# A hybrid attention, Mamba and FP4 feed-forward block on one core: set-up merged with the first front, and two products added on GpSimd in 22 of 64 scan units

## The reference, cut to what matters

```python
x = x + attn_a(_layernorm(x))     # 16 heads, latent width 32, rope, causal softmax
x = x + ffn(_layernorm(x))        # gate, up, down (704 wide), rows and weights in FP4 blocks of 16
x = x + attn_b(_layernorm(x))     # two state-space scans (forward, backward), merge, gate
x = x + ffn(_layernorm(x))
# attn_b, one direction; 512 inner channels, 16 states:
dA = exp(dt[..., None] * A);  dBu = dt[..., None] * B_ssm[:, :, None, :] * xc[..., None]
h = dAt * h + dBut                # scan over the 512 tokens, for each channel and state
y = einsum('bdn,bn->bd', h, ct)   # product with C, summed over the 16 states
```

## Time and profile before

| | us |
|---|---|
| median of the runs | 4221.96 |
| the profiled execution | 4215.24 |
| its span, first to last instruction | 4213.5 |
| TensorE busy | 3521.7 (84%) |
| VectorE busy | 3054.1 (72%) |
| ScalarE busy | 2036.8 (48%) |
| GpSimd busy | 1927.2 (46%) |
| first scan starts at | 427.6 |
| mean granted TensorE clock | 0.948 |

### The profile page before, as it was taken

One profiled execution on the slowest core, in us unless ns is written; L12 is line 12 of the kernel. 1 busy time (PEld: TensorE's weight loads), 2 busy tenths in 40 slices (PEclk: granted clock), 3 DMA queues, 4 the chain that ended last, 5 costly groups with the idle time before them and its releaser, 6 DMA issues.

```text
span 4213.5 us, 41483 instructions
## 1 busy us (share of the span) xinstructions
PE 3521.7 (84%) x13488; PEld 1871.2 (44%) x13488; DVE 3054.1 (72%) x4294; ACT 2036.8 (48%) x3852; POOL 1927.2 (46%) x1154
## 2 busy tenths in 40 slices
PE   5886798789988898879988899888988899879657
PEld 5553354245543454435543455434544355434214
DVE  3243768877687867877788776878678777887993
ACT  0354464635645455534655346544555346463441
POOL 0100744546444454445545464544544454453760
PEclk9997899999999999999999999999999999999998
DMA  3002544744446444364436444464454645364780
GB/s 84 1 1 79 190 148 130 248 166 159 142 139 237 143 142 165 137 231 138 152 133 214 157 162 147 143 233 137 136 167 147 220 143 156 128 219 145 268 275 5
DMA packets 203816, 649.64 MB, mean 154 GB/s; under 512 B 34253, under 2 KB 45520, under 8 KB 197456
## 3 DMA queue, kind: packets, MB, share of 16 engines
q1 hardware_dynamic: 203600, 646.98, 45.8%
HBM read 595.52 MB, written 51.38 MB: 154 GB/s over the span
## 4 chain that ended last, share of the span: by engine, by line
PE 48%; DVE 17%; issue 17%; ACT 11%; POOL 6%; SPq 1%; DMA 1%; POOLq 0%; DVEq 0%; ACTq 0%
PE banks L1268 18%; PE banks L1512 9%; DVE banks L844 7%; PE banks L1449 6%; PE banks L1297 5%; PE banks L1273 5%; ACT banks L1234 4%; DVE sb_arena L851 4%; PE banks L1425 3%; POOL sb_arena L980 3%; DVE sb_arena L772 2%; ACT sb_arena L1017 2%; SPq L427 1%; POOL sb_arena L892 1%; ACT sb_arena L1020 1%
## 5 line engine op out<-in xcount | busy, mean ns | idle before, releaser
L980 POOL TENSOR_TENSOR sb_arena<-sb_arena 128x1024 f32<-128x1024 f32 x512 | 1210.2, 2365 | 807.6 <-PE banks L1512 543.6
L844 DVE TENSOR_TENSOR_SCAN banks<-banks,sb_arena 128x512 f32<-128x512 f32 x1024 | 1197.9, 1215 | 212.3 <-ACT banks L1234 163.2
L1512 PE MATMUL banks<-sb_arena,sb_ident 128*128 128x512 f32 x2048 | 1041.0, 636 | 335.4 <-DVE sb_arena L851 266.0
L1234 ACT ACTIVATE banks<-sb_arena,sb_neg_a 128x512 f32<-128x512 f32 x1024 | 665.3, 682 | 1062.1 <-DVE sb_arena L851 1053.5
L1512 PEld LDWEIGHTS banks<-sb_arena,sb_ident 128*128 128x128 f32 x2048 | 386.6, 201 | 824.4 <-DVE sb_arena L851 434.1
L1017 ACT ACTIVATE sb_arena<-banks 128x512 f32<-128x512 f32 (+4 forms) x752 | 381.1, 519 | 582.8 <-PE banks L1273 389.1
L851 DVE TENSOR_TENSOR sb_arena<-banks,sb_arena 128x512 f32<-128x512 f32 x1024 | 650.5, 676 | 0.0
L1273 PE MATMUL banks<-sb_ident,sb_arena 128*128 128x128 f32 (+1 forms) x2082 | 343.8, 287 | 219.3 <-ACT sb_arena L1017 85.6
L1273 PEld LDWEIGHTS banks<-sb_ident,sb_arena 128*128 128x128 f32 (+1 forms) x2082 | 244.2, 145 | 429.7 <-ACT sb_arena L1017 156.7
L723 DVE TENSOR_REDUCE sb_nmax<-banks 128x1 f32<-128x512 f32 (+3 forms) x352 | 222.9, 636 | 290.9 <-PE banks L1452 289.4
L1449 PE MATMUL banks<-sb_arena 128*128 128x384 f32 (+3 forms) x1024 | 358.7, 461 | 0.7 <-issue 0.7
(11 more groups left out here) (126 smaller groups left out, 4027.3 us busy)
## 6 DMA issues: line engine op xcount, KB each, us to landing
sb_arena<-rows_bc SPq DMA_DIRECT2D x1024, 512.0 KB, 4.5
kept_xc<-sb_arena SPq DMA_DIRECT2D x16, 1024.0 KB, 5.0
kept_z<-sb_arena SPq DMA_DIRECT2D x16, 1024.0 KB, 4.4
sb_arena<-kept_z SPq DMA_DIRECT2D x64, 256.0 KB, 5.0
sb_arena<-kept_xc SPq DMA_DIRECT2D x64, 256.0 KB, 4.9
kept_zs<-sb_arena SPq DMA_DIRECT2D x8, 1024.0 KB, 6.6
sb_arena<-kept_zs SPq DMA_DIRECT2D x8, 1024.0 KB, 9.7
sb_xin<-in_x SPq DMA_DIRECT2D x8, 512.0 KB, 7.6
```

Of the source, the lines that this page charges most:

```text
L844: v.tensor_tensor_scan(factors, factors, products, 0.0, ALU.mult, ALU.add).then_inc(V.sem, V.mark("scan", K, e))
L980: nc.gpsimd.tensor_tensor(dBu[K % SLOTS], u[:, p % 2].unsqueeze(1).to_broadcast([P, 2, T]), rows_b[K % BS], ALU.mult).then_inc(G.sem, G.ma ...
L1234: nc.scalar.activation(psum[:, e], dt[:, (K // NQ) % 2], ACT.Exp, scale=neg_a[:, s, m, 2 * q + e:2 * q + e + 1]).then_inc(A.sem, A.mark("d ...
L1512: mm = pe.matmul(psum[:, YB], ident[:, :], dBu[K % SLOTS][:, e], start=(q == 0 and e == 0), stop=(q == NQ - 1 and e == 1))
```

## The change

**Set-up.** SyncE issues 19 loads for the folding at once, without waiting for the memsets, on a semaphore of their own (`s_fold`), then `xin`, then 18 loads that the front needs (`s_mid`: feed-forward weights, rope tables and others), then the rest (`s_w`). The folding uses all 128 rows: `rep16` repeats the 16-row latent matrices eight times down the partitions, `heads_of` keeps each head's own block, and with these block-diagonal right sides (`bd`, `bdv`) eight matmuls of 512 columns and four of 128 replace the 160 small ones; three that make the repeated matrices come ahead, and the 32 for the biases stay. The front begins behind the folding and `s_mid`. VectorE and GpSimd do one weight tile, then four visits of the front, six times; TensorE and ScalarE transpose and copy the feed-forward weights after the front's attention, bank by bank, and then do the front's feed-forward and preparation.

**Units 21 to 42 of each batch** (`ADDED`). VectorE still makes both products. GpSimd then adds the second to the first (`add_states`, after the unit's first place of visits), and TensorE waits for that sum and does one matmul instead of two. `SHARED` is empty, so the paths under `shared(K)` are never taken.

**The table** `VISITS` has new numbers: merge 10 places, ffn2 14, latents 16, attention 44, ffn1 11, early 14, late 19; 128 places in all, where there were 123. The visits' contents and their order are the same.

```diff
+ADDED, SHARED = range(21, 43), ()
-    "lat": (1, 2, 2, 2, 1, 0, 3, 2, 4, 2, 0, 2, 0, 5, 0),
-    "att": (0, 2, 2, 1, 1, 1, 2, 1, 0, 3, 1, 0, 2, 1, 4, 4, 1, 0, 0, 2, 1, 1,
-            0, 3, 0, 2, 0, 4, 1, 1, 2, 1, 3, 1, 0, 4, 1, 2, 3, 0, 1, 3, 0, 0, 3),
+    "lat": (4, 0, 0, 5, 0, 1, 1, 2, 1, 1, 5, 0, 2, 3, 0, 1),
+    "att": (0, 3, 2, 0, 2, 0, 2, 0, 4, 0, 3, 0, 2, 1, 0, 1, 2, 1, 1, 2, 2, 2,
+            0, 0, 5, 0, 4, 0, 3, 0, 1, 2, 1, 0, 4, 1, 2, 2, 0, 3, 4, 0, 0, 3),
...
         def _(sp):
+            for dst, src in fold_loads:
+                sp.dma_start(dst, src, allow_slow_non_contiguous=True).then_inc(s_fold, 16)
+            sp.dma_start(xin[:, :, :], x_dram[0]).then_inc(s_xin, 16)
             sp.wait_ge(V.sem, V.at("cleared"))
+            for dst, src in mid_loads:
+                sp.dma_start(dst, src, allow_slow_non_contiguous=True).then_inc(s_mid, 16)
             for dst, src in loads:
                 sp.dma_start(dst, src, allow_slow_non_contiguous=True).then_inc(s_w, 16)
...
+            front = beside(None, 0)
+            advance(front, MERGE_N + 1)
+            v.wait_ge(s_mid, MID)
+            v.wait_ge(A.sem, A.at("w_v"))
             for i in range(3 * CK):
...
+                advance(front, 4)
+            advance(front, LAT_N + ATT_N - 1 - 4 * 3 * CK)
+            v.wait_ge(s_w, LOADED)
...
+            def add_states(K):
+                g.wait_ge(V.sem, V.at("hc", K, 1))
+                nc.gpsimd.tensor_tensor(dBu[K % SLOTS][:, 0], dBu[K % SLOTS][:, 0], dBu[K % SLOTS][:, 1], ALU.add
+                                        ).then_inc(G.sem, G.mark("pair", K))
...
                     advance(side, visits[2 * k])
+                    if added(K):
+                        add_states(K)
...
-                for e in range(2):
-                    pe.wait_ge(V.sem, V.at("hc", K, e))
+                if added(K):
+                    pe.wait_ge(G.sem, G.at("pair", K))
+                last = 0 if added(K) else 1
+                for e in range(last + 1):
...
                     mm = pe.matmul(psum[:, YB], ident[:, :], dBu[K % SLOTS][:, e],
-                                   start=(q == 0 and e == 0), stop=(q == NQ - 1 and e == 1))
+                                   start=(q == 0 and e == 0), stop=(q == NQ - 1 and e == last))
...
-                        for h in range(H):
-                            last = q == 7 and h == H - 1
-                            accumulate(psum[:, (1 + q) % 8, h * L:h * L + L],
-                                       [(wat[:, w * H + h, k * P:k * P + P], qk17[0:HD, w, r * L:r * L + L])],
-                                       *(("w_lat",) if last else ()))
+                        accumulate(psum[:, fold_bank(w, h, k)],
+                                   [(wat[:, CK * w + h, k * P:k * P + P], bd[w].rearrange("p h l -> p (h l)"))],
+                                   "w_lat", w, h, k)
...
+            front = beside(None, 0)
+            advance(front, MERGE_N + LAT_N + ATT_N)
             pe.wait_ge(G.sem, G.at("wq", 2 * CK - 1))
```

More of the change, by code:

```diff
@@ L302, in hybrid_block @@
         lob = area(HD, rows=1)
+        rep16, heads_of = area(P, rows=HD), area(HPC)
+        bd, bdv = [area(HPC, 2 * L), area(HPC, 2 * L)], area(HPC, HD)
         a_log = area(2, DT * DS)
@@ L373, in hybrid_block @@
             ]
[L374 removed]
+        FOLD, MID, LOADED = 16 * len(fold_loads), 16 * len(mid_loads), 16 * len(loads)
         def by_block(ap):
@@ L397, in unit, with added, shared @@
             return b, p, q, p // DT, p % DT
+        def added(K):
+            return K % NU in ADDED
+        def shared(K):
+            return K % NU in SHARED
         def tile_at(t):
@@ L843, in _ @@
                         v.wait_ge(A.sem, A.at("dA", K, e))
-                        v.tensor_tensor_scan(factors, factors, products, 0.0, ALU.mult, ALU.add
-                                             ).then_inc(V.sem, V.mark("scan", K, e))
+                        v.tensor_tensor_scan(products if e == 1 and shared(K) else factors, factors, products, 0.0,
+                                             ALU.mult, ALU.add).then_inc(V.sem, V.mark("scan", K, e))
                     advance(side, visits[2 * k])
-                    for e in range(2):
+                    for e in range(1 if shared(K) else 2):
                         if e == 0:
@@ L987, in _ @@
                                         ).then_inc(G.sem, G.mark("wq", i))
-            drain(beside(None, 0))
+                advance(front, 4)
+            drain(front)
             soft_sums(0)
@@ L1175, in beside @@
                     yield from prep(n)
+            a.wait_ge(s_fold, FOLD)
+            nc.scalar.activation(b_qk[:, :], b_qk[:, :], ACT.Copy, scale=SCALE).then_inc(A.sem, A.mark())
+            for w in range(2):
+                for h in range(2):
+                    for k in range(CK):
+                        a.wait_ge(E.sem, E.at("w_lat", w, h, k))
+                        for r in range(2):
+                            at = h * HPC * L
+                            copy(w_lat[w][r][:, k, at:at + HPC * L].rearrange("p (h l) -> p h l", l=L),
+                                 psum[:, fold_bank(w, h, k)].rearrange("p (h r l) -> p r h l", h=HPC, r=2)[:, r],
+                                 "w_lat", w, h, k)
+            for k in range(CK):
+                a.wait_ge(E.sem, E.at("w_v", k))
+                copy(w_v[:, k], psum[:, 3 + k, 0:C])
+            a.wait_ge(E.sem, E.at("b_lat"))
+            copy(b_lat[:, :], psum[:, 5, 0:4 * MT])
+            a.wait_ge(E.sem, E.at("b_v"))
+            copy(b_v, psum[0:1, 6, 0:C], "w_v")
+            front = beside(None, 0)
+            advance(front, MERGE_N + LAT_N + ATT_N)
             a.wait_ge(s_w, LOADED)
@@ L1231, in factors @@
                     a.wait_ge(G.sem, G.at("edge", K // NQ))
-                if K >= 1:
+                if K >= 1 and e == 1 and shared(K - 1):
+                    a.wait_ge(V.sem, V.at("scan", K - 1, e))
+                elif K >= 1:
                     a.wait_ge(V.sem, V.at("hc", K - 1, e))
@@ L1509, in state_sum @@
                     pe.wait_ge(V.sem, V.at("ycat", g - 1))
-                for e in range(2):
-                    pe.wait_ge(V.sem, V.at("hc", K, e))
+                if added(K):
+                    pe.wait_ge(G.sem, G.at("pair", K))
+                last = 0 if added(K) else 1
+                for e in range(last + 1):
+                    if e == 1 and shared(K):
+                        pe.wait_ge(G.sem, G.at("hc", K))
+                    elif not added(K):
+                        pe.wait_ge(V.sem, V.at("hc", K, e))
@@ new lines, in _ @@
+            pe.wait_ge(A.sem, A.at("w_v"))
+            pe.wait_ge(s_mid, MID)
+            front = beside(None, 0)
+            advance(front, MERGE_N + LAT_N + ATT_N)
+            pe.wait_ge(G.sem, G.at("wq", 2 * CK - 1))
+            for k in range(CK):
+                for i in range(2 * F // P):
+                    c = i // 4
+                    if k >= 1 and i % 4 == 0:
+                        pe.wait_ge(A.sem, A.at("w_gu", k - 1, c))
+                    turn(psum[:, c, (i % 4) * P:(i % 4) * P + P], rows_gu[:, i * C + k * P:i * C + k * P + P],
+                         *(("w_gu", k, c) if i % 4 == 3 or i == 2 * F // P - 1 else ()))
@@ L1559, in _ @@
             pe.wait_ge(A.sem, A.at("set_up"))
-            accumulate(psum[0:17, 7, 0:1], [(e16[:, :], ones[0:1, 0:1])], "set_up")
-            drain(beside(None, 0))
+            pe.wait_ge(s_w, LOADED)
+            drain(front)
             for b in range(B):
```

168 lines of the change are left out of this document (94 added, 74 removed).

## The result

The changed kernel takes 3973.69 us, the median of four runs (3971.57 to 3975.25); the kernel before, run beside it, 4220.5 (4218.95 to 4224.25). The ratio is 0.9414, with a 95% interval of 0.9397 to 0.943. So 247 us are gained where 140 were forecast, and the time lies under the low end of the range, 3990.

What follows compares the result with a forecast made beforehand. TensorE was taken to bound attention, VectorE the bare units, and the head to add its time directly. Gains 88 + 4 + 54 - 6 = 140 us took the median from 4222 to 4082, range 3990 to 4145.

Steps and rivals of the forecast that it cites:

- the head: Set-up and front: faster loads and folding bring the first scan from 427.64 to about 340, 88 us earlier (75 to 98).
- the table: Same visits in 128 places instead of 123: merge stays TensorE-bound, feed-forward VectorE-bound; counted nothing, bounds -5 and +5 a batch.
- the addition: Units 21 to 42: GpSimd's addition replaces one matmul; 54 gained in batches 1 to 6, 4 in batch 0, 6 lost last.
- The attention units: Units 21 to 42, batches 1 to 6: 0.88 us matmul saved against 1.4 us delay; net 9 us a batch.
- the whole 0.88 is gained: Attention units with visits in the second place: TensorE comes later, so no wait; 11 x 0.88 us a batch.
- Batch 0: Attention stands in units 13 to 34, so only 14 of the 22 units save TensorE time: 4 us gained.
- The last batch: Bare units 21 to 42: GpSimd needs 34.3 us per group of eight, more than VectorE; 6 us lost.
- B: Rival in attention: the new wait eats what the matmul gives, batches 0 to 6 unchanged; 4140 us, chance 0.20 (clock included).
- B's second form: Attention's clock falls from 0.98 to 0.88, TensorE's work grows by 14 us a batch; 4166 us, within B's 0.20.
- C: Rival: TensorE's whole time comes out in attention and the table gains 2 us a batch; 3993 us, chance 0.12.
- D: Rival: additions stand behind `make_dBu` on GpSimd, TensorE waits 2.9 us net in every added unit; 4580 us, chance 0.03.
- E: Rival in the head: front waits for loads or tiles stretch it, so 88 becomes 50; 4120 us, chance 0.07.

Runs made afterwards that it cites:

- e2: The changed kernel without GpSimd's addition in any unit, so new head and new table only: 3986.57 us.
- e6: The changed kernel without GpSimd's addition or the wait for it, the product of state 0 left out of the sum in units 21 to 42: 3948.11 us.
- e1: The changed kernel with no addition in any unit and the old table of visits, so the new head alone: 4117.33 us.
- e15: New head, old table, no addition (e1), with all attention visits but the last moved one place, half a unit, later: 4153.11 us.
- e16: New head, new table, no addition (e2), with the attention list likewise one place later: 4242.22 us.
- e3: The changed kernel with the old table of visits, so new head and GpSimd's addition in units 21 to 42: 4146.48 us.
- e8: The changed kernel with the addition made by VectorE, right behind the unit's products, instead of by GpSimd: 4123.55 us.

## Why the prediction was wrong

By the medians, the 247 us are 103 for the head, 131 for the table and 13 for the addition. The forecast of 140 was 88 for the head, nothing for the table and 52 for the addition (4 + 54 - 6). The misses are 15, 131 and -39: the table's was by far the largest, and the addition's hid a part of it.

**The head** (forecast 88, measured 103) was right in its main path, with one step the other way round: the folding ended at 23 and the second group of loads at 26, so the loads set the front's start, where the forecast had the folding do it. Loads and folding were both sized too large: tile 0 at 26.2 instead of 35, since the fold loads landed near 10, not 16 to 17 (SyncE issues one in about 0.4 us, while the forecast took 0.78, the mean over 61 loads of all sizes), and the second group by 26, not 31. From tile 0 to the first score it took 55.2 us against a forecast of 57.3. The 34 transposes with their copies gave back 1.9, not 6: from the first score to the first scan 240.9 us before, 242.8 after. 8.8 + 2.1 + 4.1 = 15 is the miss, all three terms in the same direction.

**The attention units** look right and are not. Forecast 9 a batch, measured 11.7; but e2 shows 7.8 of these as the table's, and the addition gives 3.7. That the two numbers are near is luck. The forecast delay of the sum, 1.4 us behind the second product, held. In unit 31 of batch 3 of the changed kernel (its entry was (3, 0) in the earlier trace rows and is (0, 0) in the new table), the products, the addition and the sum are

```profile
1912.14 1.27 DVE L897 TENSOR_TENSOR sb_arena<-banks,sb_arena 128x512 f32<-128x512 f32 x2
...
1913.49 1.26 POOL L1037 TENSOR_TENSOR sb_arena<-sb_arena 128x512 f32<-128x512 f32 x1 [1.25 <-DVE sb_arena L897]
...
1914.81 1.12 PE L1592 MATMUL banks<-sb_arena,sb_ident 128*128 128x512 f32 x2 [1.33 <-POOL sb_arena L1037]
```

and the sum starts 1.40 to 1.50 after the second product's end in all eleven units in which TensorE idles for it (0.6 to 1.9 each, forecast 0.75; 1.33 in unit 31, as TensorE came there almost with the second product and the 0.65 of slack in the earlier trace rows was gone). Eight of the eleven are among the ten (x, 0) units and the bare one, three (26, 39, 41) have visits in the second place. The waits come to 11.7, under the 15 that the forecast set as its limit. The term that failed is "the whole 0.88 is gained" for units with visits in the second place: it took TensorE to be the bound throughout. e6 measures that with no wait at all: 22 matmuls, 15.7 us of TensorE, are 6.1 of time, 0.28 a unit instead of 0.88.

**The table** is the step that failed: "I count nothing", with bounds of 5 a batch. It is worth 18 a batch and 131 of the 247 us, and from e1 to e2 it shows in three places: attention (7.8; TensorE's waits for ScalarE's copies fall from 10.5 to 4.8), the units behind it (VectorE's waits for `dBu` and factors fall from 9.7 to 2.7 in units 48 to 56), and units 0 to 12 (3.0). The reason given, that merge is bound by TensorE and feed-forward by VectorE, was read from busy shares. Yet the earlier trace rows had batch 3 at 490.1 with PE 431.55 and DVE 377.92: 58 us in which TensorE, the busiest engine, was idle, and a clock of 0.88 in the preparation stretch. The gain should have been bounded by those idle microseconds and what a higher clock gives back, not by 5. The loss has no such bound: e15 shows that a shift by half a unit lengthens attention by 6 us a batch in the old table, e16 by 36 in the new one. That alone goes beyond the bounds taken.

**Batch 0** (forecast 4, measured 15.4) missed mainly for the same reason: 8.2 come with the table (e1 to e2), 7.1 with the addition, for which the 4 stood. **The last batch** (6 lost, 5.3 lost) is again two terms that cancel partly: the new merge and feed-forward lists give 3.8 (e1 to e2), the addition costs 8.8 (e2 to after). The forecast had the pace right: 34.3 us of GpSimd for a group of eight units, and 96.6 for 23 units are 33.6. It put the loss on scans that wait for `make_dBu`; these waits are 0.2, and it is the sum at the group's end that is late.

**The rivals.** B, that the wait eats the gain, is false for the new table and true for the old one: e3 is 29 slower than e1 and has the sign of B's second form, a clock under 0.95 in attention (0.94). C, the nearest in number (3993), rested on TensorE's whole time coming out, which e6 refutes. The sign that the forecast named for it, batches under 475, is there (467.8), but the table made it: the sign could not tell the two apart. D, that additions stand behind `make_dBu`: TensorE waited at most 1.9 for one beside attention; in the last batch's bare units it waited up to 3.9, and 8.8 us came of it. E, a slow head, is refuted by e1. The cause that decided, a table that takes out idle time of its own, was in no rival beyond C's 2 us a batch.

## What to carry to other kernels

A change of an interleaving table is a change of its own, however small its diff: bound its gain by the idle time of the busiest engine in each stretch, not at zero, and look at which half of a scan unit each group of visits falls in. Take a compound change apart on the chip before crediting the part with the clearer mechanism: here the matmul saved (0.88 us of TensorE) was worth 0.28 a unit of attention without any wait and 0.17 with the addition and its wait, in a stretch in which TensorE was busy 94%, and on the old table the exchange was a loss. Its parts don't add up either, so take them out singly and together. In this kernel such an exchange (an addition on another engine for a matmul) paid only in units in which TensorE arrived late anyway, gave nothing in the others, and cost 9 us in bare units.

## What the runs showed of the hardware

In e8 a VectorE addition of two SBUF tiles of 128x512 took 0.69 us alone and 2.87 beside a GpSimd operation that reads SBUF, while products with one input in PSUM stayed within 664 to 694 ns in the same run. The handoff from VectorE's product to GpSimd's addition took 0.08 us, and from there to TensorE 0.06 (0.05 in the earlier trace rows). TensorE's granted clock followed such edits: 0.55 where half of the matmuls were taken from bare units and it waited for GpSimd ahead of each, 0.94 there with them; 0.91 in attention where waits for ScalarE came to 27 us, and 1.00 where they were 5, with 10% of TensorE's time between the two.
